# A graph attention layer on one core: inverse deviation from ScalarE's square root and VectorE's reciprocal, and a later fill of the scatter table

## Chip, cores and metric

One core of a Trainium2 chip runs the whole kernel. The metric is device time in microseconds (us), the median of three runs; lower is better.

## What is computed

12500 nodes with 128 features, 412500 edges sorted by destination, 64 features per edge. The nodes go through a layer norm and a ReLU, then a graph attention with 4 heads of 32, whose result is added to the input:

```python
def _layernorm(x, axis=-1, eps=1e-05):
    m = jnp.mean(x, axis=axis, keepdims=True)
    v = jnp.var(x, axis=axis, keepdims=True)
    return (x - m) / jnp.sqrt(v + eps)

h = jnp.maximum(_layernorm(x, axis=-1), 0.0)
x = x + gnn(h, edge_index, edge_attr_64, W_node, W_edge, a)

# inside gnn
h = (node_features @ W_node.T).reshape(num_nodes, H, HD)
e = (edge_features @ W_edge.T).reshape(num_edges, H, HD)
att = jnp.sum(jnp.concatenate([h[src], h[tgt], e], axis=-1) * a, axis=-1)
att = jnp.where(att > 0, att, 0.2 * att)
m = jnp.maximum(segment_max(att, tgt), 0.0)
ex = jnp.exp(att - m[tgt])
denom = segment_sum(ex, tgt) + (num_edges - deg)[:, None] * jnp.exp(-m)
h_prime = segment_sum((ex / denom[tgt])[:, :, None] * h[src], tgt)
```

## The kernel before

The work has three stages, one behind the other on GpSimd (POOL), which issues every indirect transfer.

**Preparation.** Each partition owns 98 nodes (W) and, later, 3224 consecutive edges (T). Two things run side by side.

- *Where does each node's list of edges begin?* ScalarE finds for each of the 99 node columns a coarse chunk number in 11 batches of 9 (`count_chunks`, L362 to L366). POOL gathers for each column one row of 806 destinations into a ring of 8 buffers (L306 to L311); gather k waits until VectorE has counted in buffer k-8 (`chunk_used`). VectorE counts the entries below the node's number (`count_within`, L446). After k == 60 it also builds the table of segment borders `pen_a` (L479 to L482). From the counts it makes the index lists (L487 to L505), among them `put_i`, where each node's target term belongs in the edge list.
- *Node rows.* In 14 groups of 7 columns (STEPS, NG), TensorE centres the transposed input (`centring`, L704, which raises `centre_done`), ScalarE squares it and applies the ReLU (L378, L379), and TensorE sums the squares (L714). VectorE turns the sums into `var_s` in two halves (`variance`, L451): the first in the middle of the counting (k == 80), the second behind it. POOL raises `var_s` to the power -0.5 in two halves (`rstd_of`, L301 to L304, called at L312 and L313, behind its 99 gathers). TensorE projects a group (L721) and VectorE scales it by `rstd` into a row buffer (`project_copy`, L456 to L470), which raises `rows_ready`; SP stores it into `rows_scratch` (L242). TensorE starts its next group when `rows_ready` has risen.

The **scatter table** `tdst_scratch` has to hold -2^126 everywhere before the nodes' terms are scattered into it. SP fills it with four transfers of 1612 KB each out of a constant tile (L236 to L238, in `eab`), after the loads of the inputs and without another wait; the load of the first edge indices comes behind them (L239).

**Scatter.** POOL waits for the four fills (`tdst_filled`, L314) and the index list (`put_ready`, L315), and then scatters 98 columns of target terms, 7 for each `rows_ready` (L316 to L320). SP reads the table back into `big` when all scatters are done (L250 to L253).

**Main loop.** 248 blocks of 13 edges per partition. POOL issues 13 gathers of node rows for a block into one of 4 slots (L327 to L334); VectorE makes the logits and the running maximum (L540), multiplies and scans (L568); ScalarE takes the exponentials (L399, L401) and copies the state out (L412); SP stores it. A tail joins the partitions, gathers 98 columns of states (L347 to L352) and adds the result to x.

Of the kernel before, what the change touches and what calls it, by code (L numbers as in the profile page):

```python
# [4 lines left out]
P = 128  # L5
# [31 lines left out]
def graph_attention_kernel(nc, x, x_t, src, dstf, dst16, lasts, ends, first, ea, w_node, w_node_t, a_blk, we2,  # L37
# [13 lines left out]
    with ctx:  # L51
        def sb(name, shape, dt):
            return ctx.enter_context(nc.sbuf_tensor(name, shape, dt))
# [4 lines left out]
        def sem(name):  # L58
            return ctx.enter_context(nc.semaphore(name))
# [37 lines left out]
        rest = sb("rest", [P, W], fp32)  # L97
        tnode = sb("tnode", [P, W, H], fp32)
        rstd = sb("rstd", [P, W], fp32)
        var_s = sb("var_s", [P, W], fp32)  # L100
        minus_half = sb("minus_half", [P, W], fp32)
        ones = sb("ones", [P, 1], fp32)
# [38 lines left out]
            sem("loaded_w"), sem("loaded_ends"), sem("loaded_dst"), sem("loaded_lasts"))  # L141
        filled, tdst_filled, zeroed, zero_stored = sem("filled"), sem("tdst_filled"), sem("zeroed"), sem("zero_stored")
        half_done, w_done, w_copied, consts = sem("half_done"), sem("w_done"), sem("w_copied"), sem("consts")
        centre_done, squared, var_done, var_copied, rstd_done, projected, rows_ready = (
            sem("centre_done"), sem("squared"), sem("var_done"), sem("var_copied"), sem("rstd_done"),
            sem("projected"), sem("rows_ready"))
        rows_stored = [sem(f"rows_stored{k}") for k in range(2)]
        chunk_ready, chunk_dma, chunk_used = sem("chunk_ready"), [sem(f"chunk_dma{k}") for k in range(RING)], sem("chunk_used")
# [73 lines left out]
        def _(sp):  # L222
# [9 lines left out]
            sp.dma_start(first_i[:, :], first).then_inc(loaded_ends, 16)  # L232
            sp.wait_ge(zeroed, 1)
            sp.dma_start(state_d[P * T:P * T + 1, :], zero_row[:, :]).then_inc(zero_stored, 16)
            sp.wait_ge(filled, 1)
            td_rows = tdst_d[0:P * T, :].rearrange("(p t) h -> p (t h)", p=P)  # L236
            for k in range(H):
                sp.dma_start(td_rows[:, k * T:(k + 1) * T], fill).then_inc(tdst_filled, 16)  # L238
            sp.dma_start(idx[:, 0, :], src[:, 0:SLOTS * KB]).then_inc(idx_dma[0], 16)  # L239
            for g in range(STEPS):  # L240
                sp.wait_ge(rows_ready, g + 1)
                sp.dma_start(rows.rearrange("(p w) r -> p w r", p=P)[:, g * NG:(g + 1) * NG, :], row_t[g % 2]).then_inc(rows_stored[g % 2], 16)  # L242
# [45 lines left out]
        @block.gpsimd  # L288
        def _(pool):
            def gather(buf, table, index, done):  # L290
                pool.indirect_dma_start(buf, None, table, bass.IndirectOffsetOnAxis(ap=index, axis=0)).then_inc(done, 16)  # L291

            def scatter(table, index, buf, done):
                pool.indirect_dma_start(table, bass.IndirectOffsetOnAxis(ap=index, axis=0), buf, None).then_inc(done, 16)  # L294

            nc.gpsimd.memset(minus_half[:, :], -0.5)
            pool.drain()
            pool.wait_ge(loaded_lasts, 32)
            nc.gpsimd.tensor_tensor(half_n[:, :], cols[:, 0:W + 1], minus_half[:, 0:1].broadcast_to([P, W + 1]), ALU.add).then_inc(half_done, 1)

            def rstd_of(part):  # L301
                a, b = part * W // 2, (part + 1) * W // 2
                pool.wait_ge(var_copied, part + 1)
                nc.gpsimd.tensor_tensor(rstd[:, a:b], var_s[:, a:b], minus_half[:, a:b], ALU.pow).then_inc(rstd_done, 1)  # L304

            for k in range(W + 1):  # L306
                if k % 9 == 0:
                    pool.wait_ge(chunk_ready, k // 9 + 1)
                if k >= RING:
                    pool.wait_ge(chunk_used, k - RING + 1)  # L310
                gather(ring[:, k % RING, :], dst16[:, :], chunk_i[:, k:k + 1], chunk_dma[k % RING])  # L311
            rstd_of(0)  # L312
            rstd_of(1)  # L313
            pool.wait_ge(tdst_filled, 64)  # L314
            pool.wait_ge(put_ready, 1)  # L315
            for g in range(STEPS):  # L316
                pool.wait_ge(rows_ready, g + 1)
                for n in range(NG):
                    k = g * NG + n
                    scatter(tdst_d[:, :], put_i[:, k:k + 1], tnode[:, k, :], scattered)  # L320
            pool.wait_ge(loaded_ends, 32)
            pool.wait_ge(tnode_stored, 16)
            gather(t_first[:, :], tnode_d[:, :], first_i[:, 0:1], first_dma)
            for k in range(2):
                pool.wait_ge(rows_stored[k], 16 * (STEPS // 2))

            def body(it, q):  # L327
                s = q % SLOTS
                if s == 0:
                    pool.wait_ge(idx_dma[q // SLOTS], it * 16 + 16)  # L330
                after(pool, val_done, it * UN + q - SLOTS + 1)
                pool.sem_inc(slots_taken, 1)  # L332
                for j in range(KB):
                    gather(slots[:, s * KB + j, :], rows[:, :], idx[:, q // SLOTS, s * KB + j:s * KB + j + 1], gather_dma[s])  # L334

            loop(pool, body)

            pool.wait_ge(rest_stored, 16)
            gather(x_first[:, :], x[:, :], first_i[:, 0:1], first_dma)
            gather(rest_first[:, :], rest_d[:, :], first_i[:, 0:1], first_dma)  # L340
            pool.wait_ge(flags_done, 1)
            pool.wait_ge(zero_stored, 16)
            for k in range(2):
                pool.wait_ge(store_dma[k], 16 * (BLOCKS // 2))
            pool.wait_ge(val_done, BLOCKS)
            gather(s_first[:, :], state_d[:, :], fe_i[:, 0:1], fix_gather)
            for g in range(STEPS):  # L347
                if g >= 7:
                    pool.wait_ge(group_done, g - 6)
                for n in range(NG):  # L350
                    k = g * NG + n
                    gather(slots[:, k % 49, :], state_d[:, :], get_i[:, k:k + 1], get_dma[g])  # L352
            pool.wait_ge(fix_ready, 1)
            pool.wait_ge(stored, 16 * STEPS)
            scatter(out[:, :], fix_i[:, 0:1], x_first[:, :], fix_dma)

        @block.scalar
        def _(act):
# [16 lines left out]
            def node_step(g):  # L375
# [2 lines left out]
                nc.scalar.activation(sq[g % 2], centred[g % 2], ACT.Square)  # L378
                nc.scalar.activation(hT[:, g * NG * P:(g + 1) * NG * P], centred[g % 2], ACT.Relu).then_inc(squared, 1)  # L379

            count_chunks(0)
            copy_weights()
            for g in range(STEPS):
                node_step(g)
                if g < 10:
                    count_chunks(g + 1)

            act.wait_ge(pen_a_done, 1)
            act.wait_ge(pen_set, 1)
# [43 lines left out]
        def _(dve):  # L433
# [17 lines left out]
            def variance(part):  # L451
                a, b = part * W // 2, (part + 1) * W // 2
                dve.wait_ge(var_done, 7 * (part + 1))
                nc.vector.tensor_scalar(var_s[:, a:b], var_p[part], 1.0 / D, EPS, ALU.mult, ALU.add).then_inc(var_copied, 1)

            def project_copy(g):  # L456
                dve.wait_ge(projected, g + 1)
                dve.wait_ge(rstd_done, 1 if g < 7 else 2)
                after(dve, rows_stored[g % 2], 16 * (g // 2))
                for a, b, bank in proj:  # L460
                    v = bank[:, 0:(b - a) * WE].rearrange("p (w r) -> p w r", r=WE)
# [11 lines left out]
            for k in range(W + 1):  # L473
# [8 lines left out]
                    nc.vector.tensor_scalar(pen_a[:, :], pen_a[:, :], 2.0 * BIG, -BIG, ALU.mult, ALU.add).then_inc(pen_a_done, 1)  # L482
                if k == 80:
                    variance(0)
            variance(1)
            dve.drain()
            nc.vector.tensor_copy(cnt[:, :], chunk_i[:, :])  # L487
            dve.drain()
# [14 lines left out]
            nc.vector.tensor_tensor(pick[:, :], pick[:, :], none_f[:, :], ALU.mult)  # L503
            dve.drain()
            nc.vector.scalar_tensor_tensor(get_i[:, :], cnt[:, 1:W + 1], -1.0, pick[:, :], ALU.add, ALU.add)  # L505
            for g in range(STEPS):
                project_copy(g)

# [297 lines left out]
```

## Time and profile before

| | |
|---|---|
| median of 3 runs | 4519.24 us (4519.19 to 4522.25) |
| profiled execution, its own time | 4519.71 us |
| its span, first to last instruction | 4517.7 us |
| POOL busy | 3382.6 us (75% of the span) |
| VectorE (DVE) busy | 2492.8 us (55%) |
| ScalarE (ACT) busy | 1366.4 us (30%) |
| TensorE (PE) busy | 819.8 us (18%) |
| DMA | 139 GB/s over the span |

A row of a timeline reads: start in us, duration in us, engine, line, operation, tile written <- tile read, number of instructions merged, and in brackets how long the engine had idled before it and who ended that. Starts are counted from the first instruction. A group row gives busy us and mean ns of one, then the idle time just before the group's instructions and its releasers; "issue" is a gap in which the engine waited for nothing that the profile shows. Matmul ends are modelled.

### The profile page before, as it was taken

To read this page: it belongs to the slowest core of one execution; us is meant where nothing else is said; L and a number is where in the kernel's file an instruction comes from. 1 tells how busy PE (TensorE), PEld (TensorE's weight loads), DVE (VectorE), ACT (ScalarE), POOL (GpSimd) and SP (SyncE) were. 2 spreads that over 40 slices of the span, in tenths; PEclk is the share of its full clock that TensorE was granted. 3 is DMA by queue.
4 is the path that set the end of the run, shared out by engine and by line. 5 is a ranking of instruction groups with operands and counts; after the bars stand their busy time and mean duration, and the time that the engine had idled before them with its cause. 6 is when DMAs were issued, how large, how long until landed. Compare 5 with 4: busy or idle time off the path is not lost.

```text
span 4517.7 us, 21382 instructions
## 1 busy us (share of the span) xinstructions
PE 819.8 (18%) x3685; PEld 777.8 (17%) x3685; DVE 2492.8 (55%) x3230; ACT 1366.4 (30%) x1008; POOL 3382.6 (75%) x3532
## 2 busy tenths in 40 slices
PE   6301111112121211111121212121111112121200
PEld 4301111111111111111111111111111111111100
DVE  7516555555555555555555555555555555555553
ACT  8103333333333333333333333333333333333320
POOL 6777777777777777777777777777777777777756
PEclk6655555555555555555555555555555555555555
DMA  7424444444444444444444444444444444444453
GB/s 265 131 90 136 138 134 141 130 141 135 142 135 142 135 142 135 138 139 132 138 134 142 135 142 135 142 134 142 135 134 140 130 141 135 142 135 142 134 171 97
DMA packets 189542, 627.98 MB, mean 139 GB/s; under 512 B 74865, under 2 KB 75634, under 8 KB 188882
## 3 DMA queue, kind: packets, MB, share of 16 engines
q0 software_dynamic: 115936, 252.37, 23.3%
q1 hardware_dynamic: 73586, 375.40, 22.5%
q8 instruction: 5, 0.08, 0.0%
q14 instruction: 15, 0.12, 0.0%
HBM read 382.66 MB, written 244.86 MB: 139 GB/s over the span
## 4 chain that ended last, share of the span: by engine, by line
POOL 72%; issue 24%; DMA 1%; DVE 1%; PE 0%; POOLq 0%; ACT 0%; DVEq 0%; SPq 0%; ACTq 0%
POOL slots L291 70%; POOL tdst_scratch L294 1%; DMA V<-in_dst_dram,chunk_i 1%; POOL V L291 1%; DVE pen L448 1%; PE ae L721 0%; DVE slots L463 0%; POOL rstd L304 0%; POOLq L173 0%; DVE V L571 0%; ACT pen L364 0%; DMA rows_scratch<-slots 0%; DMA state_scratch<-R 0%; POOLq L332 0%; DVE V L581 0%
## 5 line engine op out<-in xcount | busy, mean ns | idle before, releaser
L291 POOL DMA_INDIRECT slots<-rows_scratch,idx x3224 | 3076.0, 954 | 982.4 <-issue 982.4
L732 PE MATMUL ae<-w_att,eab 128*128 128x8 f32 x3224 | 707.0, 361 | 3375.0 <-DVE z L550 3373.2
L732 PEld LDWEIGHTS ae<-w_att,eab 128*128 128x128 f32 x3224 | 696.3, 331 | 3385.8 <-DVE z L550 2433.3
L581 DVE TENSOR_TENSOR_SCAN V<-A,V 128x1848 f32<-128x1848 f32 x248 | 993.6, 4007 | 18.1
L401 ACT ACTIVATE A<-D 128x1848 f32<-128x1848 f32 x248 | 425.1, 1714 | 1849.3 <-DVE V L581 1849.3
L545 DVE TENSOR_TENSOR z<-slots,big 128x52 f32<-128x52 f32 x248 | 62.3, 251 | 1567.4 <-DMA slots<-rows_scratch,idx 1567.4
L412 ACT COPY R<-V 128x1768 f32<-128x1768 f32 x248 | 791.1, 3190 | 2.8 <-DVE V L581 2.8
L571 DVE TENSOR_TENSOR V<-slots,wexp 128x1716 f32<-128x1716 f32 x124 | 401.6, 3239 | 13.8
L571 DVE TENSOR_TENSOR V<-slots,extra 128x1716 f32<-128x1716 f32 x124 | 400.5, 3230 | 13.7
L399 ACT ACTIVATE wexp<-D 128x52 f32<-128x52 f32 x124 | 27.0, 218 | 562.5 <-DVEq L566 562.5
L399 ACT ACTIVATE extra<-D 128x52 f32<-128x52 f32 x124 | 27.0, 218 | 475.4 <-DVEq L566 475.4
L291 POOL DMA_INDIRECT V<-in_dst_dram,chunk_i x99 | 96.8, 977 | 45.3 <-issue 23.5
L448 DVE TENSOR_SCALAR_CACHE_REDUCE pen<-V,cols 128x806 bf16<-128x806 int16 x99 | 101.6, 1051 | 36.9 <-DMA V<-in_dst_dram,chunk_i 34.8
L294 POOL DMA_INDIRECT tdst_scratch<-tnode,put_i x98 | 94.8, 967 | 29.8 <-issue 29.4
L291 POOL DMA_INDIRECT slots<-state_scratch,get_i x98 | 93.2, 951 | 29.9 <-issue 29.9
L557 DVE TENSOR_TENSOR_SCAN V<-pen,att 128x56 f32<-128x56 f32 (+1 forms) x248 | 72.8, 294 | 47.9 <-issue 45.8
L564 DVE SCALAR_TENSOR_TENSOR D<-pen,dm 128x52 f32<-128x52 f32 (+1 forms) x248 | 52.9, 213 | 40.9 <-issue 40.3
L578 DVE COPY V<-V 128x132 f32<-128x132 f32 x247 | 75.0, 304 | 0.0
L364 ACT ACTIVATE pen<-last_b,half_n 128x512 bf16<-128x512 f32 x99 | 69.9, 713 | 0.0
L550 DVE TENSOR_TENSOR z<-z,ae 128x52 f32<-128x52 f32 x248 | 51.7, 208 | 27.6 <-issue 4.9
L554 DVE SCALAR_TENSOR_TENSOR att<-z 128x52 f32<-128x52 f32 x248 | 52.7, 213 | 22.9
L562 DVE COPY att<-V 128x4 f32<-128x4 f32 x248 | 64.8, 261 | 0.0
(148 smaller groups left out, 535.2 us busy)
## 6 DMA issues: line engine op xcount, KB each, us to landing
state_scratch<-R SPq DMA_DIRECT2D x248, 884.0 KB, 4.2
eab<-in_ea_dram SPq DMA_DIRECT2D x126, 832.0 KB, 6.3
slots<-rows_scratch,idx POOLq DMA_INDIRECT x3224, 2.6
rows_scratch<-slots SPq DMA_DIRECT2D x14, 476.0 KB, 2.5
tdst_scratch<-eab SPq DMA_DIRECT2D x4, 1612.0 KB, 30.9
big<-tdst_scratch SPq DMA_DIRECT2D x8, 806.0 KB, 10.9
big<-in_x_t_dram SPq DMA_DIRECT2D x14, 448.0 KB, 8.3
big<-in_x_dram SPq DMA_DIRECT2D x7, 896.0 KB, 11.8
```

The source lines that it names most:

```text
L291: pool.indirect_dma_start(buf, None, table, bass.IndirectOffsetOnAxis(ap=index, axis=0)).then_inc(done, 16)
L294: pool.indirect_dma_start(table, bass.IndirectOffsetOnAxis(ap=index, axis=0), buf, None).then_inc(done, 16)
L364: nc.scalar.activation(junk_a[k % 9], last_b[:, :], ACT.Sign, bias=half_n[:, k:k + 1], scale=-1.0, accum_out=sgn[:, k:k + 1])
L401: nc.scalar.activation(a_all.rearrange("p (h v t) -> p h v t", h=H, v=HB), D2[:, v, :].rearrange("p (h a t) -> p h a t", h=H, a=1).broadca ...
L412: nc.scalar.copy(R[:, k, :, :], vcols(k)[:, :, 1:COL].rearrange("p c t -> p t c")).then_inc(copied, 1)
L448: nc.vector.tensor_scalar(junk_v[k % RING], ring[:, k % RING, :], cols[:, k:k + 1], None, ALU.is_lt, ALU.add, accum_out=within[:, k:k + 1] ...
L557: nc.vector.tensor_tensor_scan(mcols(v), pen[:, ds(i, 1), :, :].rearrange("p a h t -> p (a h t)"), att[:, :], 0.0, ALU.min, ALU.max)
L562: nc.vector.tensor_copy(hk(att[:, :])[:, :, 0:1], hk(mcols(v))[:, :, KB:COL])
L571: nc.vector.tensor_tensor(v4[:, :, :, 1:COL], slots[:, s * KB:(s + 1) * KB, 0:VAL].rearrange("p t (h v) -> p h v t", h=H), w_exp[k].rearra ...
L578: nc.vector.tensor_copy(vcols(k)[:, 0:VAL, 0:1], vcols(1 - k)[:, 0:VAL, KB:COL])
L581: nc.vector.tensor_tensor_scan(V[:, k, 0:VAL * COL], a_all, V[:, k, 0:VAL * COL], 0.0, ALU.mult, ALU.add).then_inc(scanned, 1)
L732: last = mm(ps_ae[k][:, n * 2 * H:(n + 1) * 2 * H], eab[:, k, n * P:(n + 1) * P], w_att[:, :], start=True, stop=True)
```

## The change

`std` is a new tile of 128 x 98 numbers. POOL's two powers are gone. ScalarE takes the square root of each half of `var_s` (`deviation`) behind its last node step, before it waits for `pen_a_done`. The second `variance` moves into the counting, behind k == 93. VectorE makes the reciprocal of `std` behind the last index list and refines it once: r * (1.5 - 0.5 * r * r * var). The wait on the power in `project_copy` is gone. On SP, the load of the first edge indices goes ahead of the fills, and fill k (0 to 3) waits until `centre_done` has reached 8 + k.

```diff
+        std = sb("std", [P, W], fp32)
...
+            td_rows = tdst_d[0:P * T, :].rearrange("(p t) h -> p (t h)", p=P)
+            sp.dma_start(idx[:, 0, :], src[:, 0:SLOTS * KB]).then_inc(idx_dma[0], 16)
             sp.wait_ge(filled, 1)
-            td_rows = tdst_d[0:P * T, :].rearrange("(p t) h -> p (t h)", p=P)
             for k in range(H):
+                sp.wait_ge(centre_done, 8 + k)
                 sp.dma_start(td_rows[:, k * T:(k + 1) * T], fill).then_inc(tdst_filled, 16)
-            sp.dma_start(idx[:, 0, :], src[:, 0:SLOTS * KB]).then_inc(idx_dma[0], 16)
...
-            def rstd_of(part):
-                a, b = part * W // 2, (part + 1) * W // 2
-                pool.wait_ge(var_copied, part + 1)
-                nc.gpsimd.tensor_tensor(rstd[:, a:b], var_s[:, a:b], minus_half[:, a:b], ALU.pow).then_inc(rstd_done, 1)
-
             for k in range(W + 1):
...
-            rstd_of(0)
-            rstd_of(1)
             pool.wait_ge(tdst_filled, 64)
...
+            def deviation(part):
+                a, b = part * W // 2, (part + 1) * W // 2
+                act.wait_ge(var_copied, part + 1)
+                nc.scalar.activation(std[:, a:b], var_s[:, a:b], ACT.Sqrt).then_inc(std_done, 1)
+
             count_chunks(0)
             copy_weights()
             for g in range(STEPS):
                 node_step(g)
                 if g < 10:
                     count_chunks(g + 1)
+            deviation(0)
+            deviation(1)
...
             def project_copy(g):
                 dve.wait_ge(projected, g + 1)
-                dve.wait_ge(rstd_done, 1 if g < 7 else 2)
...
                 if k == 80:
                     variance(0)
-            variance(1)
+                if k == 93:
+                    variance(1)
...
             nc.vector.scalar_tensor_tensor(get_i[:, :], cnt[:, 1:W + 1], -1.0, pick[:, :], ALU.add, ALU.add)
+            dve.wait_ge(std_done, 2)
+            nc.vector.reciprocal(rstd[:, :], std[:, :])
+            dve.drain()
+            nc.vector.tensor_tensor(std[:, :], rstd[:, :], rstd[:, :], ALU.mult)
+            dve.drain()
+            nc.vector.tensor_tensor(std[:, :], std[:, :], var_s[:, :], ALU.mult)
+            dve.drain()
+            nc.vector.tensor_scalar(std[:, :], std[:, :], -0.5, 1.5, ALU.mult, ALU.add)
+            dve.drain()
+            nc.vector.tensor_tensor(rstd[:, :], rstd[:, :], std[:, :], ALU.mult)
+            dve.drain()
             for g in range(STEPS):
                 project_copy(g)
```

## Rows read from the trace of the kernel before

**Rows 1.** The page: POOL's gathers of the main loop, costliest groups.

```profile
L291 POOL DMA_INDIRECT slots<-rows_scratch,idx x3224 | 3076.0, 954 | 982.4 <-issue 982.4
```

**Rows 2.** Timeline of POOL: first and last gather of preparation, powers, scatter, main loop's start.

```profile
12.91 1.12 POOL L291 DMA_INDIRECT V<-in_dst_dram,chunk_i  x1 [7.97 <-ACT chunk_i L366]
...
146.04 0.95 POOL L291 DMA_INDIRECT V<-in_dst_dram,chunk_i  x1 [0.30 <-issue]
147.02 16.38 POOL L304 TENSOR_TENSOR rstd<-var_s,minus_half 128x49 f32<-128x49 f32 x2
163.59 1.04 POOL L294 DMA_INDIRECT tdst_scratch<-tnode,put_i  x1 [0.18 <-issue]
...
289.53 0.96 POOL L291 DMA_INDIRECT slots<-rows_scratch,idx  x1 [0.30 <-issue]
```

**Rows 3.** Timeline of POOL: two gathers of preparation off the regular pace.

```profile
33.34 0.95 POOL L291 DMA_INDIRECT V<-in_dst_dram,chunk_i  x1 [0.53 <-DVE pen L448]
...
100.64 3.80 POOL L291 DMA_INDIRECT V<-in_dst_dram,chunk_i  x1 [0.30 <-issue]
```

**Rows 4.** Who waited for whom, POOL, 42 to 58 us: total, times, longest.

```profile
POOL V L291 <- DVE pen L448: 9.4, 7, 1.8
```

**Rows 5.** DMA queues, 42 to 57 us: packets, MB, share of 16 engines.

```profile
q1 hardware_dynamic: 474, 3.66, 58.4%
q0 software_dynamic: 728, 2.33, 41.1%
```

**Rows 6.** DMA queues, 60 to 99 us; q1 moved nothing.

```profile
q0 software_dynamic: 1987, 6.41, 62.0%
```

**Rows 7.** Page, DMA issues: number, KB of one, median us to landing.

```profile
tdst_scratch<-eab SPq DMA_DIRECT2D x4, 1612.0 KB, 30.9
```

**Rows 8.** Timeline of TensorE: centring of groups 7 and 10.

```profile
57.40 3.33 PE L704 MATMUL A<-big,centre 128*128 128x512 f32 x4
...
83.47 3.33 PE L704 MATMUL A<-big,centre 128*128 128x512 f32 x4
```

**Rows 9.** Timeline of VectorE: border table, last count, index lists, first and last scaled group.

```profile
99.71 3.51 DVE L479 TENSOR_TENSOR pen_a<-R 128x3223 bf16<-128x3223 f32 x1
...
149.15 1.05 DVE L448 TENSOR_SCALAR_CACHE_REDUCE pen<-V,cols 128x806 bf16<-128x806 int16 x1
150.13 0.20 DVE L454 TENSOR_SCALAR var_s<-wexp 128x49 f32<-128x49 f32 x1
150.42 0.21 DVE L487 CAST cnt<-chunk_i 128x99 f32<-128x99 int32 x1
...
152.97 0.26 DVE L503 TENSOR_TENSOR pick<-pick,none_f 128x98 f32<-128x98 f32 x1
153.31 0.26 DVE L505 SCALAR_TENSOR_TENSOR get_i<-cnt,pick 128x98 int32<-128x98 f32 x1
155.35 0.56 DVE L463 TENSOR_TENSOR slots<-ae,rstd 128x384 f32<-128x384 f32 x1 [1.78 <-POOL rstd L304]
...
156.86 0.15 DVE L469 TENSOR_TENSOR tnode<-wexp,rstd 128x4 f32<-128x4 f32 x1
...
209.97 0.15 DVE L469 TENSOR_TENSOR tnode<-wexp,rstd 128x4 f32<-128x4 f32 x1
```

**Rows 10.** Groups of VectorE by form, 4300 to 4520 us: both reciprocals.

```profile
L680 DVE RECIPROCAL wexp<-R 128x28 f32<-128x28 f32 x14 | 4.7, 336 | 1.0
...
L664 DVE RECIPROCAL R<-R 128x4 f32<-128x4 f32 x1 | 0.2, 178 | 0.1
```

**Rows 11.** Groups of ScalarE by form: the one table load of the run.

```profile
L364 ACT ACT_TABLE_LOAD x1 | 1.3, 1283 | 4.6 <-DMA cols<-in_cols_dram 4.6
```

**Rows 12.** Timeline of ScalarE: what follows its node steps, then the first exponential.

```profile
214.48 11.48 ACT L391 ACTIVATE pen<-pen_a 128x3224 bf16<-128x3224 bf16 x4 [107.73 <-DVE pen L509]
...
312.81 0.22 ACT L399 ACTIVATE wexp<-D 128x52 f32<-128x52 f32 x1 [86.85 <-DVEq L566]
```

**Rows 13.** Timeline of VectorE: the first product of the main loop.

```profile
330.79 3.20 DVE L571 TENSOR_TENSOR V<-slots,wexp 128x1716 f32<-128x1716 f32 x1
```

More of the change, by code:

```diff
@@ L143, in graph_attention_kernel @@
         half_done, w_done, w_copied, consts = sem("half_done"), sem("w_done"), sem("w_copied"), sem("consts")
-        centre_done, squared, var_done, var_copied, rstd_done, projected, rows_ready = (
-            sem("centre_done"), sem("squared"), sem("var_done"), sem("var_copied"), sem("rstd_done"),
+        centre_done, squared, var_done, var_copied, std_done, projected, rows_ready = (
+            sem("centre_done"), sem("squared"), sem("var_done"), sem("var_copied"), sem("std_done"),
             sem("projected"), sem("rows_ready"))
```

## The prediction, made before the changed kernel was run

> **What bounds the kernel now.** I read the page's costliest groups first. The 3224 gathers of the main loop take 3076.0 us on POOL, and all of POOL's idle time before them, 982.4 us, is "issue": no data and no other engine is ever waited for [rows 1]. 3076.0 + 982.4 = 4058 us, 90% of the 4517.7 us span. The change touches nothing in that loop. What it can move is the moment at which the loop begins, 289.53 us, and everything behind that follows rigidly.
>
> So I followed POOL's timeline backward from there [rows 2]. The first scatter is at 163.59; 98 scatters and one small gather fill 289.53 - 163.59 = 125.94 us, 1.272 us each with no exception. In front of them two powers hold POOL for 16.38 us, and they start 0.03 us after the last gather of the preparation: `var_s` was ready, the powers only had to wait for their place in POOL's queue. In front of them stand 99 gathers from 12.91 to 146.04, 133.13 us for 98 steps. A regular step is 0.95 + 0.30 = 1.25 us, 122.6 us for 98. The other 10.5 us are in four places: 0.17 us at the first gather; 0.23 at 33.34 and 3.80 - 0.95 = 2.85 at 100.64 [rows 3]; and, seven times between 42 and 58 us, a wait for VectorE to free a ring buffer, 9.4 us with 7 x 0.30 of ordinary gap in it, so 7.3 us lost [rows 4]. In that stretch the DMA engines are full: SP's queue takes 58.4% of them and POOL's 41.1% [rows 5], where the gathers at full pace want 62.0% [rows 6]. What SP's queue moves there is the table's fill, whose four transfers land 30.9 us (median) behind their issue [rows 7]. The fills starve the gathers, VectorE gets its columns late, the ring of 8 is full, and POOL stands.
>
> Two prices on one chain, then: 7.3 us of starved gathers and 16.4 us of powers.
>
> **The change, part by part.**
>
> *The fills move behind `centre_done` 8 to 11.* The stall between 42 and 58 us goes. In its place come four separate fills. TensorE ends the centring of group 7 at 57.40 + 3.33 = 60.7 and that of group 10 at 83.47 + 3.33 = 86.8, so they are issued about 8.7 us apart [rows 8]; this schedule is set by ScalarE's batches and stays. What does one fill do to the gathers? 3.66 MB took 58.4% of 15 us [rows 5], which is 2.39 us of all engines for a MB; a fill of 1612 KB (1.65 MB) is 3.95 us of work, and at a share of 58.4% it lasts 6.8 us. Meanwhile gathers run at 41.1 / 62.0 = 66% of their pace and fall 2.3 us behind. In the 1.9 us until the next fill they have all engines, 1 / 0.62 = 1.61 times their pace, and win back 1.2 us. After four fills the lag is 4 x 2.3 - 3 x 1.2 = 5.6 us. The ring bears 8 x 1.25 = 10.0 us from one gather's start to the end of its count; the last one needed 149.15 - 146.04 = 3.1 us to arrive and 1.05 to be counted [rows 2, 9], so 5.9 us are spare. 5.6 is just inside. But near 92 to 97 us VectorE comes to k == 60 and leaves the ring alone for at least the 3.51 us of the border table [rows 9], while POOL itself is held for 2.85 [rows 3]; that adds 0.7 us or a little more to the lag at its worst moment. I price the new stall at 0.5 us and keep 0 and 4 us as its bounds; the far end, all 7.3 us, is a rival. The 2.85 us at the border table stay, by the phase of the two engines 1 us more or less.
>
> The Trainium skill ("DMA: Bandwidth & Descriptors", Queues, rings and completion order) says that a DMA engine takes turns between queues by packet. The packets of rows 5 are 3.66 MB / 474 = 7.7 KB against 3.2 KB, and by that rule the fills would get 71%, not the 58.4% that was measured. One fill would then last 5.6 us and cost 3.0 us of lag, four of them end near 6 us, and the stall would be 1 to 2 us, the forecast later by about one. The row decides for the sum.
>
> SP's queue: the edge indices are loaded earlier, and nobody needs them before the main loop. The fills now wait, and behind them in SP's queue stands the first store of node rows, which before came when the first group was scaled, at 157 us [rows 9]. The last fill is issued at 87 and lands before 100; at the worst landing per fill of today, about 31 us [rows 7], at 118. It holds neither the stores nor POOL's wait at L314.
>
> *The powers go from POOL.* That takes 16.38 us out of its queue, and now its scatter waits for `rows_ready`, which has a new chain of its own. Counted from the start of the last gather [rows 2, 9]:
> - the count starts at +3.11, as now; the cast of L487 started at 150.42, +4.38. With `variance(1)` (0.20 us) moved ahead of it: +4.18.
> - the index lists until L505: 153.31 - 150.42 = 2.89, +7.07. The reciprocal follows 0.2 us later, +7.27.
> - the reciprocal on 98 columns is not in the trace. On 28 columns it takes 336 ns and on 4 columns 178 ns [rows 10]. The lower bound is the 0.26 us of any operation on 98 columns [rows 9]; the upper is 0.336 x 98 / 28 = 1.18. The slope of the two rows gives 0.336 + 70 x 0.0066 = 0.80, and I take that, with 0.1 us until the next starts: +8.17.
> - four more operations with a drain each, at 153.31 - 152.97 = 0.34 a step [rows 9]: 1.36, +9.53. Between bounds that is 8.9 to 9.9; today's scaling starts at 155.35, +9.31. VectorE's refinement is as long as POOL's first power was.
> - scaling of the first group: from 155.35 to 156.86 + 0.15, 1.66 us, +11.19, and 0.1 us to POOL: +11.3.
>
> Today the first scatter stands at +17.55. What was late there was the second power (147.02 + 16.38 = 163.40), for which no scatter of the first group needed to wait. What is late next is `rows_ready`. Later groups do not hold POOL either: 14 groups are scaled between 156.86 and 209.97, 4.1 us a group [rows 9], against 7 x 1.272 = 8.9 us of scattering.
>
> *ScalarE takes the square roots.* It sits idle for 107.73 us, until 214.48 [rows 12], and the second half of `var_s` comes at k == 93, more than 6 us before the counts end. Two short operations and a table load of 1.28 us (the size of the one in the trace [rows 11]) fit twice over: nothing. Without this cover it would be some 2 us on the chain. A switch back to the exponentials' table is due before the first exponential, at 312.81 today; its product is first used at 330.79 [rows 12, 13], so 18 us of slack cover it. Should a load stand in every pass of the loop, one in 8 blocks, it meets an engine that is busy 30% of the time. The skill ("ScalarE: Activation LUTs", What ACT_TABLE_LOAD costs) warns of this very pattern: exponential and square root lie in different sets, and each switch costs about 2.7 us with its drain. Two of them exposed would take 5.3 us off the gain; the rows say that none is.
>
> **The sum.** The last gather starts at 146.04 - 7.3 + 0.5 = 139.2, the first scatter at 139.2 + 11.3 = 150.5 instead of 163.6: 13.0 us. Behind it nothing changes. The profiled execution took 4519.71 us, 4517.7 of it span; it becomes 4506.7, its span 4504.7. It lies 0.5 us above the median of 4519.24, so I forecast 4506.2 us.
>
> **The rivals.**
>
> *The fills keep their price.* They starve the gathers at 61 to 95 us as they did at 42 to 58, and the border table comes on top. For it: the engines' total demand in this stretch is 3.95 + 8.7 x 0.62 = 9.3 us of work in 8.7 us, more than there is, and my margin is 5.9 against 5.6. Against it: before, the ring was already full when the fills began (the wait at 33.34), now the DMA queue is empty at 60 us. With all 7.3 us back and my 0.5 out: 13.0 + 0.5 - 7.3 = 6.2 us gained, 4513.0. With half back, 4509.5.
>
> *POOL is not freed.* The scatter stays near 163.6 because something else is late: the first group's projection, or the square root. TensorE may start once k == 93 is counted, 6 us before the last count, and needs some 4 us. I see nothing that lasts 12 us. The time would be 4519.
>
> *The loop's pace.* The one thing large enough to make the kernel slower is POOL's own issue gap: 3224 gathers with 982.4 us of gap, 0.305 us each [rows 1]. The POOL program gets shorter and all its instructions move. If the gap grew by more than (13.0 + 9.0) / 3224 = 7 ns, the kernel would be slower by over 0.2%; 10 ns would give 4538. For it speaks only that nothing in the profile explains the gap. Against it: the same gap of 0.30 us stands in all three stages of POOL's queue [rows 2, 3].
>
> *More than that.* With a milder border table and no new stall, 14 to 16 us: 4503 to 4505.
>
> **How the numbers follow.** The forecast's case (11 to 15 us gained) gets 0.70, the fills' return 0.17, POOL not freed 0.04, the loop's pace 0.05, more than 15 us 0.04. A measurement of this kernel can tell about 0.2%, 9 us, from no change. Faster by more: 0.70 + 0.04 and a third of the fills' case, 0.80. Within: the rest of it and POOL not freed, 0.15. Slower: 0.05. The range, 4503.5 to 4512.5, takes in the reciprocal's bounds (0.5 us either way), the border table's phase (1 us) and a new stall of up to 6 us; it leaves out the full return of the stall and the last three cases.
>
> **What the changed profile would show.** No POOL row of L304; the waits of POOL on the counts gone between 42 and 58 us, and under 1 us beyond the ordinary gap between 60 and 100; last preparation gather near 139, reciprocal near 146.5 with about 0.8 us, first scatter near 150.5, main loop near 276.5; two table loads more on ScalarE, neither with a waiter. The prediction is wrong if the ring is full for several us behind the fourth fill, if `rows_ready` comes much later than 11.3 us behind the last gather, or if the 4058 us of the main loop change.

## The result and the profile after

| | before | after |
|---|---|---|
| median | 4519.22 us | 4481.91 us (4481.47 to 4482.77) |
| ratio | | 0.9916 (95% interval 0.9899 to 0.9933) |
| profiled execution | 4519.71 us | 4481.47 us |
| its span | 4517.7 us | 4479.6 us |

The kernel became 37.3 us faster where 13.0 were forecast: the direction was right, the size was not, and 4481.9 lies far below the range that I had given. (The median before is that of four executions; the 4519.24 us further up is that of three.)

POOL's timeline after the change, from the last gather of the preparation to the main loop's start. It answers to [rows 2].

```profile
12.79 1.10 POOL L293 DMA_INDIRECT V<-in_dst_dram,chunk_i  x1 [7.96 <-ACT chunk_i L361]
...
138.26 0.95 POOL L293 DMA_INDIRECT V<-in_dst_dram,chunk_i  x1 [0.30 <-issue]
...
150.25 0.99 POOL L296 DMA_INDIRECT tdst_scratch<-tnode,put_i  x1 [11.05 <-DVE tnode L470]
...
276.41 0.96 POOL L293 DMA_INDIRECT slots<-rows_scratch,idx  x1 [0.30 <-issue]
```

The loop begins at 276.41 instead of 289.53: 13.1 us, as forecast. The rest of the gain is behind this point, where I had written that nothing changes. The page's group of the main loop's gathers, which answers to [rows 1]:

```profile
L293 POOL DMA_INDIRECT slots<-rows_scratch,idx x3224 | 3051.7, 947 | 982.5 <-issue 982.5
```

The idle gap is the same to 0.1 us (982.4 before). The busy time fell from 3076.0 to 3051.7: 24.3 us in 3224 gathers, 7.5 ns each. One gather before and after, in the same stretch of the loop, from 2000 to 2500 us (duration in ns, least/median/most), first before, then after:

```profile
L291 POOL DMA_INDIRECT slots<-rows_scratch,idx x398: 947/952/996, 2000.2 to 2498.9; - x199
```

```profile
L293 POOL DMA_INDIRECT slots<-rows_scratch,idx x401: 940/944/973, 1999.6 to 2499.1; - x134
```

The whole distribution moved, its least value too, so this is no stall that went away here and there: a typical gather takes 8 ns less of POOL. The 98 gathers of the tail went the same way, from 952 to 944 ns at the median, 0.7 us. 13.1 + 24.3 + 0.7 = 38.1 us, and the spans of the two profiled executions differ by 4517.7 - 4479.6 = 38.1. Nothing is left over.

### The profile page after: what moved, and what is told of

Read it like the earlier page. It is cut to its first block, busy times and chain, and to the rows that moved or that the text cites. A ratio compares the mean times of both kernels' runs of the same rounds, so it can differ in the third digit from the quotient of the medians.

```text
span 4479.6 us, 21393 instructions
## 1 busy us (share of the span) xinstructions
PE 818.0 (18%) x3685; PEld 776.2 (17%) x3685; DVE 2494.4 (56%) x3235; ACT 1369.5 (31%) x1012; POOL 3341.1 (75%) x3530
## 4 chain that ended last, share of the span: by engine, by line
POOL 72%; issue 24%; DVE 2%; DMA 1%; POOLq 0%; ACT 0%; DVEq 0%; SPq 0%; ACTq 0%
POOL slots L293 70%; POOL tdst_scratch L296 2%; DVE pen L450 1%; DMA V<-in_dst_dram,chunk_i 1%; POOL V L293 1%; POOLq L174 0%; DVE V L584 0%; ACT pen L359 0%; DMA state_scratch<-R 0%; POOLq L327 0%; DVE V L594 0%; DVEq L609 0%; DVE pen_a L480 0%; ACT R L414 0%; DMA cols<-in_cols_dram 0%
## 5 line engine op out<-in xcount | busy, mean ns | idle before, releaser
L293 POOL DMA_INDIRECT slots<-rows_scratch,idx x3224 | 3051.7, 947 | 982.5 <-issue 982.5
L573 DVE TENSOR_TENSOR D<-att,V 128x52 f32<-128x52 f32 x248 | 53.0, 214 | 18.4
```

## The experiments

What has to be explained is a loop whose source lines the change does not touch. My first theory, P: a power that POOL has run makes its later gathers slower. The rival, L: the length of POOL's program, that is where its instructions lie, does it. A third: the later fills do it.

### The two parts, each alone

e1_fills_alone is the kernel before with SP's part of the diff; e2_roots_alone is the changed kernel with SP's part undone:

```diff
-            sp.dma_start(idx[:, 0, :], src[:, 0:SLOTS * KB]).then_inc(idx_dma[0], 16)
             sp.wait_ge(filled, 1)
             for k in range(H):
-                sp.wait_ge(centre_done, 8 + k)
                 sp.dma_start(td_rows[:, k * T:(k + 1) * T], fill).then_inc(tdst_filled, 16)
+            sp.dma_start(idx[:, 0, :], src[:, 0:SLOTS * KB]).then_inc(idx_dma[0], 16)
```

> The kernel before with SP's part of the change alone: the four fills wait for the centring of groups 7 to 10; the powers stay on POOL. Theory P (once POOL has run a power, each of its later gathers takes 8 ns more) and theory L (the length of POOL's program sets it) both expect the main loop's gathers to stay at a median of 952 ns, as before; a third theory (the later fills themselves make the loop faster) expects 944 ns. The starved gathers' 7.3 us come back: last gather of the preparation near 139.2 us, first scatter 17.5 us behind it, near 156.7. Time by P and L 4519.2 - 6.9 = 4512.3 us, by the third 4488 us.

Measured: 4512.94 us beside 4520.04 for the kernel before, the loop's gathers at 952 ns, first scatter at 156.41.

> The changed kernel with the fills where they were: the square root and the reciprocal alone. P and L expect the main loop's gathers at 944 ns; the theory of the fills expects 952. Last gather of the preparation near 146.0 us, first scatter 11.1 us behind it, near 157.1, so 6.5 us before the loop. Time by P and L 4519.2 - 6.5 - 24.3 = 4488.4 us, by the theory of the fills 4512.7.

Measured: 4489.18 us, 944 ns, first scatter at 158.18. So the fills are worth 7.1 us and the roots 30.9, together 38.0. The 24 us come with the roots; the theory of the fills falls.

### Same program, another operation

e3_mult_for_pow is the kernel before with a product in place of each power; it leaves out the inverse deviation:

```diff
-                nc.gpsimd.tensor_tensor(rstd[:, a:b], var_s[:, a:b], minus_half[:, a:b], ALU.pow).then_inc(rstd_done, 1)
+                nc.gpsimd.tensor_tensor(rstd[:, a:b], var_s[:, a:b], minus_half[:, a:b], ALU.mult).then_inc(rstd_done, 1)
```

> The kernel before with one operation code changed: POOL multiplies var_s by -0.5 instead of raising it to -0.5 (the inverse deviation is left out, so the output is not the reference's). POOL's program keeps its length and order. P expects 944 ns for the main loop's gathers, L expects 952. In front of the loop two products of some 0.3 us take the place of 16.4 us; the first scatter then waits for the first scaled group, near 155.4 us, 8.2 us earlier. Time by P 4519.2 - 8.2 - 24.3 = 4486.7 us, by L 4511.0.

Measured: 4488.21 us. POOL's timeline, and a gather of the loop:

```profile
146.84 0.30 POOL L304 TENSOR_TENSOR rstd<-var_s,minus_half 128x49 f32<-128x49 f32 x1
150.30 0.29 POOL L304 TENSOR_TENSOR rstd<-var_s,minus_half 128x49 f32<-128x49 f32 x1 [3.15 <-DVE var_s L454]
156.34 1.03 POOL L294 DMA_INDIRECT tdst_scratch<-tnode,put_i  x1 [5.76 <-DVE tnode L469]
```

```profile
L291 POOL DMA_INDIRECT slots<-rows_scratch,idx x401: 940/944/984, 1999.6 to 2499.2; - x134
```

POOL's program has the same instructions in the same order, and the gathers are at 944 ns. Between these two programs what POOL ran decides, not the program's length. A product of the same shape takes 0.30 us where a power took 8.2.

### A small power in front, and its twin

e4_pow_first is the changed kernel with this at the head of POOL's program; e5_mult_first is the same with `ALU.mult`.

```diff
             nc.gpsimd.memset(minus_half[:, :], -0.5)
+            nc.gpsimd.memset(probe[:, :], 2.0)
             pool.drain()
+            nc.gpsimd.tensor_tensor(probe[:, 0:2], probe[:, 2:4], minus_half[:, 0:2], ALU.pow)
```

> The changed kernel with a power on two columns of a new tile at the head of POOL's program, used by nobody. P expects 952 ns for the main loop's gathers, and already for the 99 gathers of the preparation 8 ns more than 946; time 4481.9 + 25.8 = 4508 us. L has no power in it: with two instructions more in front, 944 or 952 by where they fall; if it is the number of instructions that counts, 952 like before, so this run alone does not part P from L, but the next, the same with a product, does. A quick return to 944 would fell P.

> The twin of e4_pow_first: the same two instructions in front, with a product in place of the power. P (a power that has run makes the gathers slower) expects 944 ns for the main loop's gathers and 946 in the preparation, and the time of the changed kernel, 4481.9 to 4482.5 us. L (the length of POOL's program) expects what e4 showed, 952 ns and 4508 us.

Measured: 4507.96 us with the power, 4481.67 with the product. A gather of the loop in e4, then in e5:

```profile
L294 POOL DMA_INDIRECT slots<-rows_scratch,idx x399: 947/952/987, 1999.6 to 2499.7; - x200
```

```profile
L294 POOL DMA_INDIRECT slots<-rows_scratch,idx x401: 940/944/987, 2000.1 to 2499.6; - x134
```

The power itself takes 0.72 us at the start of the run, for two columns, and costs 26 us by the end; the gathers of the preparation are slower too, 953 ns against 946. So two columns do what two halves of 49 did. L falls with this pair too.

### The power behind the loop

e6_pow_behind_loop has that small power behind `loop(pool, body)`.

> The changed kernel with the same small power on POOL behind the main loop, in front of the tail's 98 gathers of states. If it is the running of the power that counts, the main loop stays at 944 ns and the tail's gathers go from 944 to 952 ns; time 4481.9 + 0.8 for them + 0.7 for the power + 0.8 = about 4483.5 us, of which part hides behind the last blocks. If it is enough that the program holds a power, the main loop goes to 952 ns and the time to 4508 us.

Measured: 4482.74 us; the loop stays at 944 ns and the tail's gathers, behind the power, are at 952:

```profile
L294 POOL DMA_INDIRECT slots<-state_scratch,get_i x98: 947/952/955, 4340.3 to 4462.1; - x98
```

### Can the mark be taken away?

e11_pow_then_others is e4 with three small instructions of other kinds behind the power:

```diff
             nc.gpsimd.tensor_tensor(probe[:, 0:2], probe[:, 2:4], minus_half[:, 0:2], ALU.pow)
+            nc.gpsimd.tensor_copy(probe[:, 4:6], probe[:, 2:4])
+            nc.gpsimd.tensor_scalar(probe[:, 6:8], probe[:, 2:4], 3.0, 1.0, ALU.mult, ALU.add)
+            nc.gpsimd.tensor_tensor(probe[:, 8:10], probe[:, 2:4], minus_half[:, 0:2], ALU.subtract)
```

> e4_pow_first with a copy, a scaled sum and a difference on POOL behind the small power. If the power's mark on the gathers lasts for the rest of the execution whatever POOL runs behind it, the main loop's gathers stay at 952 ns and the time at 4508 us. If another arithmetic instruction clears it, they go to 944 ns and the time to 4482.5.

In the batch of e10 and e11 the kernel before took 5169.47 us instead of 4520, so no time of it is compared (5176.34 for e11, 5169.4 for e10); e11's gathers were at 945 ns. e12_pow_then_others2 repeats it, and e15_pow_then_copy keeps the copy alone.

> e11_pow_then_others once more, beside an undisturbed kernel before. The mark cleared: 944 ns and 4482.5 us. The mark kept: 952 ns and 4508 us.

> The same with the copy alone behind the small power. In e4 the sum of L301 (a plain TENSOR_TENSOR) ran behind the power and did not clear the mark; of the three instructions of e11 the difference is of the same kind, so the copy or the scaled sum should have done it. Copy clears: 944 ns, 4482.4 us. Scaled sum does: 952 ns here, 4508 us.

Measured: 4482.7 us and 4481.98 us, both at 944 ns. A copy of two columns, 0.17 us, undoes what the power did. The sum that makes `half_n` (L301 of the changed kernel), which ran behind the power in e4, had not. Each of the two times is the median of two executions.

e14_before_cleared puts the same three lines into the kernel before, behind `rstd_of(1)`:

> The kernel before, powers and fills as they were, with a copy, a scaled sum and a difference on two columns of a new tile behind the second power on POOL. If these clear the power's mark on the gathers (as the 945 ns of e11 suggest), the main loop's gathers go from 952 to 944 ns with both powers in place: 4519.2 - 24.3 - 0.8 (tail) + 0.6 (three small instructions) = 4494.7 us. If the mark stays, 952 ns and 4520 us.

Measured: 4494.74 us beside 4519.84. POOL's timeline, and a gather of the loop:

```profile
146.61 16.40 POOL L306 TENSOR_TENSOR rstd<-var_s,minus_half 128x49 f32<-128x49 f32 x2
162.96 0.19 POOL L316 COPY probe<-probe 128x2 f32<-128x2 f32 x1
163.12 0.19 POOL L317 TENSOR_SCALAR probe<-probe 128x2 f32<-128x2 f32 x1
163.28 0.19 POOL L318 TENSOR_TENSOR probe<-probe,minus_half 128x2 f32<-128x2 f32 x1
163.64 1.08 POOL L295 DMA_INDIRECT tdst_scratch<-tnode,put_i  x1 [0.18 <-issue]
```

```profile
L292 POOL DMA_INDIRECT slots<-rows_scratch,idx x402: 940/944/983, 1999.1 to 2499.8; - x134
```

Three instructions of 0.19 us, which compute nothing that anyone reads, bring 25.1 us with both powers and the early fills in place.

### Is it the power at all?

In e14 the scatters moved as well, from 967 to 958 ns. The last two experiments put the three lines into the fastest kernel (below), which has no power: e16_small_ones_scatter between the last gather of the preparation and the scatter, e17_small_ones_loop between the scatter and the loop.

> e13_roots_earlier2 with the three small instructions of e14 in POOL's idle time between its last gather of the preparation and the first scatter. In e14 they stood there behind two powers and the scatters took 958 ns instead of 967 (969 without powers). If the small instructions make the scatters faster by themselves: 958 ns, 98 x 11 ns = 1.1 us, 4476.1 us. If it takes a power in front: 969 ns and 4477.2 us. The main loop's gathers stay at 944 ns by both.

> e13_roots_earlier2 with the three small instructions between the scatter and the main loop. If what POOL ran last before the loop sets the gathers' time also without a power, the main loop's gathers leave 944 ns: each ns is 3.2 us. If only a power leaves a mark and these only remove it, they stay at 944 ns and the time is 4477.2 + 0.5 us.

Measured: e16 4483.49 us, e17 4503.5 us; the kernel without them had 4477.23 in another batch. A gather of the loop in e16, then in e17:

```profile
L294 POOL DMA_INDIRECT slots<-rows_scratch,idx x401: 942/945/989, 1999.2 to 2499.5; - x134
```

```profile
L294 POOL DMA_INDIRECT slots<-rows_scratch,idx x399: 947/952/987, 1999.4 to 2499.4; - x200
```

Both expectations of e16 missed. The scatters stayed at 970 ns, yet the time rose by 6.3 us. In its profiled execution, which with 4486.68 us was the slowest of five (the others took 4483.4 to 4484.0), the loop's gathers have 8.1 us more of busy time, 2.5 ns each in the mean, and the gathers of the preparation are at 957 ns. In e17 the three lines that took the 8 ns away behind a power put them on without one. So theory P in its first form falls too: 952 ns do not need a power. The same three lines in two places give 945 and 952 ns. And e16 shows more. Its preparation, between 105 and 135 us:

```profile
L294 POOL DMA_INDIRECT V<-in_dst_dram,chunk_i x25: 952/957/960, 104.4 to 134.7; - x25
```

The three lines run at 140.74 us, and the gathers ahead of them are already at 957 ns, against 946 in e13. Either something from before this execution reaches into it, or the place of the instructions has some share after all. The first has a sign of its own in the traces. POOL's fourth instruction of all, a constant's memset 0.35 us from the start, in the kernel before and then in e3, whose programs differ in one operation code that runs 146 us later (least/median/most in ns):

```profile
L796 POOL MEMSET const-uint8-127<- x1: 93/93/93, 0.3 to 0.3; 128x1 uint8 x1
```

```profile
L796 POOL MEMSET const-uint8-127<- x1: 113/113/113, 0.3 to 0.3; 128x1 uint8 x1
```

In all eight traces of a program that holds a power this memset takes 93 to 98 ns, in the ten others 110 to 119, before a power of the same execution can have run. What carries over is not simply the loop's level, though: the kernel before, e1, e6 and e17 end at 952 ns and begin their preparation at 946. (Of which program the execution ahead of each profiled one was is not on record.) No run tells the two explanations of e16 apart.

### The stall of the starved gathers

e9_fills_together:

```diff
-                sp.wait_ge(centre_done, 8 + k)
+                sp.wait_ge(centre_done, 8)
```

> The changed kernel with all four fills waiting for the centring of group 7 only, so that they are issued one behind the other near 61 us. The theory of starved gathers: 4 x 6.8 = 27 us at 66% of the pace put the gathers 9.2 us behind, the ring bears 5.9, POOL stands for 3.3 us and some 0.7 more for the border table; 4485.9 us. If the stall of the kernel before came only because the fills stood on top of the input loads, nothing is lost: 4481.9. If fills in one piece cost what they did before, 7.3 us: 4489.2.

Measured: 4488.67 us. Who waited for whom on POOL, 73 to 88.8 us, in e9:

```profile
POOL V L293 <- DVE pen L450: 7.8, 6, 1.5
POOL V L293 <- ACT chunk_i L361: 1.4, 1, 1.4
```

Seven waits, 9.2 us less 7 x 0.30, are 7.1 us lost: the stall of [rows 4] again, 30 us later, with no input load beside it. It is the fills' being in one piece that costs, and not their meeting the loads. My own number, 3.3, was half of it. Part of the reason is in the DMA queues between 62 and 68 us, here in the changed kernel, while its first fill ran (packets, MB, share of the engines' time):

```profile
q1 hardware_dynamic: 144, 1.65, 71.9%
q0 software_dynamic: 108, 0.38, 22.5%
```

A fill takes 72% of the engines, not the 58.4% that I took from [rows 5], and the gathers fall to 22.5 / 62.0 = 36% of their pace. The kernel before had no milder split. In it, between 45 and 50 us, with the ring full:

```profile
q1 hardware_dynamic: 141, 1.61, 76.4%
q0 software_dynamic: 140, 0.47, 23.7%
```

The 58.4% are a mean over 42 to 57 us, and in the last part of that stretch the fills had run out: from 51 to 57 us SP's queue has 30.1%. The rule by packets of the Trainium skill ("DMA: Bandwidth & Descriptors", Queues, rings and completion order) fits these two rows: with both queues busy, 141 packets of one went beside 140 of the other. That the 71% which I had worked out with it are so near the 71.9% measured is luck. They were a share of bytes, from a mean packet of 7.7 KB; a fill's own packets here are larger (1.65 MB / 144 = 11.5 KB), and its share of the bytes is 1.65 / 2.03 = 81%.

### What is left in front of the scatter

In the changed profile POOL idles 11.05 us before the first scatter. e8_roots_in_counting moves VectorE's part of that into the slack between its columns:

```diff
                 if k == 80:
                     variance(0)
-                if k == 93:
                     variance(1)
+                if k == 83:
+                    dve.wait_ge(std_done, 2)
+                    nc.vector.reciprocal(rstd[:, :], std[:, :])
...
+                if k == 87:
+                    project_copy(0)
...
-            for g in range(STEPS):
+            for g in range(1, STEPS):
                 project_copy(g)
```

> The changed kernel with both halves of the variance behind k == 80, the reciprocal and its refinement behind k == 83 and the scaling of the first group behind k == 87, so that they lie in VectorE's slack between columns. My theory of the path in front of the scatter (last count, index lists, reciprocal, first group) says that 2.1 + 1.7 + 1.7 us leave it: VectorE falls 4 us behind, wins back 0.27 us a column and is level again at the last one; the first scatter waits for put_ready alone, at 144.8 instead of 150.3 us. Time 4476.4 us. The rival (VectorE's lag fills the ring and comes out on POOL's gathers) gives it all back: 4482.

Measured: 4477.43 us, first scatter at 146.86. e13_roots_earlier2 has the same steps behind k == 74, 78 and 82. It repeats e10_roots_earlier, which took 5169.40 us in the batch named above.

> e8_roots_in_counting with its three steps 5 or 6 columns earlier: both variances behind k == 74, the reciprocal and its refinement behind k == 78, the first group behind k == 82. In e8 VectorE's last count came 1.3 us late and the first scatter 0.8 us behind the index list. If VectorE's lag was what was left, it has time to win it back: the last count on time, the first scatter near 145.5 us instead of 146.9, time 4477.4 - 1.4 = 4476.0 us. If the second half of the sums is not there at k == 74 or the square roots make VectorE wait, the ring fills and the time is 4478 or more.

> e10_roots_earlier once more beside an undisturbed kernel before: last count on time, first scatter near 145.5 us, time 4476.0 us; if the square roots make VectorE wait, 4478 or more.

Measured for e13: 4477.23 us, 4.7 us less than the changed kernel; a miss of 1.2 us in the expected 4476.0. In its timelines the index list's row and the first scatter's:

```profile
145.07 0.26 DVE L514 TENSOR_TENSOR put_i<-pick,cnt 128x98 int32<-128x98 f32 x1
```

```profile
146.12 1.06 POOL L296 DMA_INDIRECT tdst_scratch<-tnode,put_i  x1 [6.49 <-issue]
```

What the expectations left out is the hand-over from `put_i` to POOL, 146.12 - 145.07 - 0.26 = 0.8 us, and a last gather that starts at 138.69 (e13) and 139.22 (e8) instead of 138.26. This second part is not the work of the moved steps: POOL's gather at the border table, near 97 us and ahead of them, took 4.00 us in e13 and 4.41 in e8 instead of 3.61, and that is nearly the whole difference. VectorE itself had caught up: its last count starts 3.33 and 3.54 us behind that gather, against 3.16 in the changed kernel. With 4477.23 and 4477.43 us, e13 and e8 are not told apart; they are the fastest kernels of the study.

## Why the prediction was wrong, point by point

**The stage in front of the loop: right, by two errors that cancel.** 13.1 us against 13.0. The chain behind the last gather, VectorE's timeline:

```profile
142.57 0.21 DVE L489 CAST cnt<-chunk_i 128x99 f32<-128x99 int32 x1
...
145.63 0.76 DVE L509 RECIPROCAL rstd<-std 128x98 f32<-128x98 f32 x1
...
147.76 0.56 DVE L464 TENSOR_TENSOR slots<-ae,rstd 128x384 f32<-128x384 f32 x1
...
149.27 0.15 DVE L470 TENSOR_TENSOR tnode<-wexp,rstd 128x4 f32<-128x4 f32 x1
```

From the last gather at 138.26 that is +4.31 for the cast (forecast 4.18), +7.37 for the reciprocal (7.27), 0.76 us for it (0.80 by the slope of [rows 10]), +9.50 for the scaling (9.53), +11.16 for its end (11.19). Then 0.83 us pass until POOL's first scatter, where I had written 0.1. In the kernel before, this hand-over was hidden behind the powers; e13 shows it again behind `put_i`. Against this stands the last gather, 0.9 us earlier than forecast: no new stall where I had put 0.5 us, 2.66 us at the border table instead of 2.85, and a first gather 0.12 us earlier (12.79).

**The fills: right in kind, wrong in the working.** The waits between 42 and 58 us are gone, and between 73 and 88.8 none is above the ordinary gap. But the step "a fill lasts 6.8 us at 58.4%" failed: 72%, landing 6.9 us after its issue (median), gathers at 36% of their pace. I had taken the split from a stretch that goes on beyond the fills; while they ran, it was 76% there too. At 72% the bytes of a fill need 6.8 x 58.4 / 72 = 5.5 us, and at 36% of their pace the gathers fall back by 5.5 x 0.64 = 3.5 us in it. A second failing step hid the first: I had let the delays of the four fills add up. VectorE's counts in the changed kernel, around the first fill:

```profile
64.23 1.05 DVE L450 TENSOR_SCALAR_CACHE_REDUCE pen<-V,cols 128x806 bf16<-128x806 int16 x1 [0.65 <-DMA V<-in_dst_dram,chunk_i]
...
68.75 1.05 DVE L450 TENSOR_SCALAR_CACHE_REDUCE pen<-V,cols 128x806 bf16<-128x806 int16 x1 [3.46 <-DMA V<-in_dst_dram,chunk_i]
...
70.90 1.05 DVE L450 TENSOR_SCALAR_CACHE_REDUCE pen<-V,cols 128x806 bf16<-128x806 int16 x1
71.87 1.05 DVE L450 TENSOR_SCALAR_CACHE_REDUCE pen<-V,cols 128x806 bf16<-128x806 int16 x1
```

From a gather's start to its count it is 3.2 us ahead of the fills (k = 37, counted from 0) and 6.9 us behind the first one (k = 39, the count at 68.75), 3.7 more. Then VectorE mostly counts every 0.97 us and wins back 0.27 a column; the delay is at 5.4 to 5.9 just before the next fills and at 7.1, 7.0 and 6.9 behind them. So a fill does not add its 3.7 us to what is left over: the DMA queue is empty by then, what is left over lies in front of VectorE, and VectorE works it off while the fill holds the gathers back. Up to the border table the worst is 3.9 us of extra delay where the ring has 5.9 to spare. In e9 there is no pause, the transfers themselves pile up, and the same delay goes 7.6, 9.7, 10.5 and on to 15.1 us. The pauses are worth 4488.67 - 4481.91 = 6.8 us.

**The table loads: right.** Neither has a waiter.

```profile
110.62 1.28 ACT L379 ACT_TABLE_LOAD   x1
120.55 0.24 ACT L379 ACTIVATE std<-var_s 128x49 f32<-128x49 f32 x1 [8.65 <-DVE var_s L456]
136.49 0.24 ACT L379 ACTIVATE std<-var_s 128x49 f32<-128x49 f32 x1 [15.69 <-DVE var_s L456]
205.07 11.49 ACT L393 ACTIVATE pen<-pen_a 128x3224 bf16<-128x3224 bf16 x4 [68.34 <-DVE pen L522]
216.57 1.28 ACT L401 ACT_TABLE_LOAD   x1
```

The square roots' load stands ahead of the wait for `var_s`, the exponentials' behind the penalty tiles, 83 us before its first user. Here the two loads cost nothing, although square root and exponential are the pair against whose mixing the Trainium skill warns ("ScalarE: Activation LUTs", Table sets: the hidden batching unit).

**"Behind it nothing changes": the step that failed, with 25.0 of 37.3 us.** The sum carried the loop's 3076.0 + 982.4 = 4058 us over as they stood, on the ground that the change touches nothing in the loop. The runs show 3051.7 + 982.5: the term left out is 3224 x 7.5 ns = 24.3 us in the loop and 0.7 us in the tail, and it came with the powers' going. A change of the 4058 us was the last of the signs of being wrong that I had named, and the place stood among the rivals: POOL's pace in the loop, where 7 ns decide over 22 us. But I looked for it in the gap between gathers, which did not move, and only upward. The direction was forecast for the 13 us in front of the loop, which came; that the other 25 went the same way was luck. The profile held a hint that I passed over: the gathers of the preparation, ahead of the powers, took 946 ns, and those of the loop, behind them, 952 at the median, on the same engine with the same instruction. Without the powers the two are at 946 and 944.

**What caused it.** Shown, each time between two programs that differ in one operation code: that taking the powers away (e3) gives the 24 us, and that putting a small one in (e4 against e5) takes 26. Measured, but with one or three instructions more in the program and no twin of equal length beside it: that a copy behind a power, alone (e15) or with two others (e14), gives them back, and that the same small instructions in another place take them without any power (e17). There the order of what POOL ran and the place of its instructions change together, and no run parts them. Not shown: what inside POOL holds this, and how it reaches ahead of the instruction in e16.

## What to carry to other kernels

Where one instruction runs thousands of times on the engine that bounds the kernel, compare its least and median duration before and behind every other kind of instruction on that engine; a shift of 1% in it outweighs the instruction that one wanted to remove. If POOL has to do arithmetic between its indirect transfers, try a small copy behind it and measure: here one copy of 0.2 us bought 26 (e15), and in another place three small instructions, 0.6 us, cost 26 (e17). And split a large transfer that runs beside a ring of small ones, with pauses in which the ring's reader can catch up: the same bytes cost 7 us in one piece and none in four.

## What the runs showed of the hardware

- One indirect gather with 128 rows takes POOL 944 or 945 ns at the median in this loop in some programs and 952 in others; 946 to 957 ns in the preparation, and a scatter 958 to 970. Between programs that differ only in a power or a product the power makes it 952 (e3, e4 and e5). Within the loop, 4 ms long, no trace shows the level move: from one 400 gathers to the next the median changes by 1 ns at most.
- POOL needs 8.2 us for a power on 49 columns and 0.72 on 2, 0.30 for a product on 49 and 0.18 on 2.
- VectorE's reciprocal on 98 columns takes 0.76 us, three times another operation of that size (0.26).
- A 1612 KB fill beside gathers took 72% of the DMA engines over the 6 us that hold it (changed kernel), and several fills in a row 76% while the gathers' ring was full (kernel before, 45 to 50 us), where the two queues moved 141 and 140 packets.
- From the end of the VectorE instruction that a waiting scatter needs to the scatter's start POOL takes 0.8 us (changed kernel, e13).
